# Four transformer layers on one core: the rotary exchange of the last layer by the vector engine's shuffle in place of four extra projections

## The chip, the core and the metric

One core of a Trainium2 chip. TensorE (PE in the profile; PEld is its weight load), VectorE (DVE), ScalarE (ACT), GpSimd (POOL) and SyncE (SP, which here only issues DMAs) run in parallel, each through its own instruction stream in program order; semaphores tie them together. Matmul results land in PSUM, which has eight banks. The metric is the device time of one execution in microseconds (us).

## The reference, cut to what matters

16 sequences of 256 tokens, 256 features, 16 heads of 16 features, go through four different transformer layers (0 to 3). All are: norm, modulation, attention, residual, norm, modulation, feed-forward, residual. Layer 3 is the only one that rotates queries and keys, and its feed-forward has two halves (gate and value), so twice the first product.

```python
def _rope(x):                       # layer 3, for q and for k, per head of 16
    ang = arange(T)[:, None] * inv_freq[None, :]
    x0, x1 = (x[..., 0::2], x[..., 1::2])
    o0 = x0 * cos - x1 * sin
    o1 = x1 * cos + x0 * sin
    return jnp.stack([o0, o1], axis=-1).reshape(x.shape)

qkv = x @ w_qkv + b_qkv
q, k, v = jnp.split(qkv, 3, axis=-1)
q = _rope(...q...); k = _rope(...k...)
attn = softmax(einsum('bhqd,bhkd->bhqk', q, k) / sqrt(hd))
out = einsum('bhqk,bhkd->bhqd', attn, v) ... @ w_ao + b_ao
...
a, gate = split(x @ w_fc + b_fc, 2); ffn = (a * silu(gate)) @ w_fo + b_fo
```

The rotation needs, for each feature, the value of its partner in the pair (2i, 2i+1).

## The kernel before

**Precision.** A product in float32 is made of three products of a high and a low part (hi*hi, hi*lo, lo*hi; the helper `product`, line L481). So each projection of 128 features (`project`) is 6 matmuls of 128x256, two 128-row pieces of the input times three. Names that end in h or l are such parts.

**Pipeline.** The unit of work is a tile: one sequence in one layer, 64 in all, layer by layer. One step t of the program works on five tiles at once, in different stages: n = t+2 (statistics and normalisation before attention), q = t+1 (norm to features, query, key and value projections), a = t (scores, softmax, outputs), r = t-1 (output projection, first residual, second norm), m = t-2 (feed-forward: `up`, activation, `down`, second residual). Every engine has a `body(s)` with the order of its work in a step written out by hand; there is no scheduler. The flag `rope` (on PE) and the tests `s.lq == ROPE` are true in the 16 steps t = 47 to 62, in which tile q is of layer 3; m is of layer 3 from t = 50 on.

**A step on PE.** First the front: eight rounds of `up(j)` and `down(j)` (feed-forward of m), with the output transposes, the output projection, and the score pairs 0 to 5 of tile a between them (a pair is two heads; L530). The front ends with `maxima_to_rows(0)` (L695). The rest of the step is called the tail here: `query`, `key`, the score pairs 6 and 7, then for eight pairs the transposed scores (`transposed_pair`, L724) which ACT turns into exponentials (L905), `values`, four groups of `outputs` (L747, each needs four heads' exponentials and the next set needs the banks that they free), and `norm_2` (transposes of the second norm, L590). Then the next step's `up(0)`.

**The rotation.** In layer 3, `query(f)` and `key(f)` project twice: once with the normal columns of the weights, once with columns in which each pair is swapped (columns 3*D and 4*D on), into banks 0 and 2 beside banks 1 and 3. `rotate` on DVE adds the biases and multiplies by cosine and signed sine (four SCALAR_TENSOR_TENSOR, L1157) into the buffer `G`; `split_rotated` adds the two products (L1168) and splits the sum into high (L1170) and low part (L1172) in `QHL` or `KHL`. SP then copies these into the stacked operands `QS` and `KS` of the scores by DMAs (L1345), 6 for each operand and group of heads. `G` is also the ring of the feed-forward's activations.

**Banks.** The bank of each head's score is in `S_BANKS`, of its transposed score in `ST_BANKS`, each with one table for layers 0 to 2 and one for layer 3, since there the swapped projections take banks 0 and 2. `NORM2_BANK` is that of `norm_2`. In the rope steps PE's transposed pair 0 writes banks 0 and 1, so it stands behind both projections and the rotation of the query, and `norm_2` waits for the rotation of the key.

**DVE in the tail**, rope steps: row maxima of the scores (`maxima`, L976, two instructions a pair), the multiplication or copy of the feed-forward's result (L1144), `rotate` of q, `statistics_2`, `split_rotated` of q, `rotate` of k, `normalise_2` (L956), `split_rotated` of k, `modulate_2` (L1094, L1100), `statistics_1` of tile n, evacuation of the outputs (L1108), `normalise_1` of n, the values (L1116).

## Time and profile before

| | |
|---|---|
| median of 3 runs | 2475.57 us (2473.37 to 2478.87) |
| profiled execution | 2480.4 us, of which span 2478.5 us |
| mean granted TensorE clock | 0.982 |
| PE / DVE / ACT / POOL busy | 93% / 66% / 51% / 44% |
| instructions | 63608 |

The profiled execution is one more run, 4.8 us above the median. The span is from its first to its last instruction. PE's busy share counts matmuls from issue to modelled end, and they overlap, so the distance between starts tells more than the share.

### The profile page before, as it was taken

How to read it: one execution, taken by the hardware profiler on the slowest of the kernel's cores; microseconds unless marked ns; L12 is line 12 of the kernel's file. 1: busy time of each engine (PE TensorE's matmuls, PEld its weight loads, DVE VectorE, ACT ScalarE, POOL GpSimd, SP SyncE). 2: the span in 40 equal slices, each digit the busy share in tenths (PEclk: the TensorE clock that was granted, in tenths of full speed). 3: DMA queues.
4: the chain of work that ended last, by engine and by line, in shares of the span. 5: the costliest groups of instructions: out<-in, count | busy, mean ns of one | idle time of the engine just before them, and what ended most of it. 6: DMA issues, size and time to landing. Idle time of an engine off the chain costs nothing.

```text
span 2478.5 us, 63608 instructions
## 1 busy us (share of the span) xinstructions
PE 2306.8 (93%) x20776; PEld 1908.5 (77%) x20776; DVE 1646.9 (66%) x3820; ACT 1255.5 (51%) x2624; POOL 1084.0 (44%) x1319
## 2 busy tenths in 40 slices
PE   6699999999999999999999999999999999999997
PEld 5477778877778778877777777777778787887876
DVE  3566676666665565556766676667777777677763
ACT  0366655566655554555666655566543433434332
POOL 1244444544544444444554444445534344343433
PEclk9799999999999999999999999999999999999988
DMA  6222121122211211122222211122221111111110
GB/s 211 84 67 69 63 61 61 59 71 80 90 63 57 66 59 51 61 69 78 86 79 67 68 57 58 60 70 84 64 82 45 63 51 50 65 42 60 52 53 14
DMA packets 165535, 166.66 MB, mean 67 GB/s; under 512 B 29392, under 2 KB 144976, under 8 KB 165424
## 3 DMA queue, kind: packets, MB, share of 16 engines
q1 hardware_dynamic: 165424, 165.21, 20.8%
q8 instruction: 65, 1.06, 0.2%
q14 instruction: 46, 0.38, 0.1%
HBM read 58.99 MB, written 4.39 MB: 26 GB/s over the span
## 4 chain that ended last, share of the span: by engine, by line
PE 47%; issue 20%; POOL 15%; DVE 10%; ACT 3%; SPq 1%; POOLq 1%; DMA 0%; DVEq 0%; ACTq 0%
PE B L481 20%; POOL GHl L1244 7%; PE B L581 7%; PE B L724 4%; PE B L530 4%; PE B L747 4%; PE B L506 3%; ACT PR L905 3%; DVE NEGM L976 2%; PE B L590 2%; POOL H1l L1283 2%; POOL X L1230 2%; POOL H2l L1270 1%; POOL X L1238 1%; PE B L600 1%
## 5 line engine op out<-in xcount | busy, mean ns | idle before, releaser
L905 ACT ACTIVATE PR<-B 128x512 f32<-128x512 f32 (+1 forms) x1024 | 508.4, 564 | 433.7 <-PE B L724 329.0
L1244 POOL TENSOR_TENSOR GHl<-G,GHh 128x256 fp32r<-128x256 f32 x512 | 376.5, 736 | 503.0 <-ACT GHh L878 332.1
L976 DVE TENSOR_REDUCE NEGM<-B 128x2 f32<-128x512 f32 x768 | 479.0, 683 | 78.7 <-PE B L530 78.0
L481 PE MATMUL B<-H2h,W1h 128*128 128x256 f32 x1280 | 394.5, 308 | 5.1 <-issue 3.1
L878 ACT ACTIVATE G<-B,VEC 128x256 f32<-128x256 f32 x384 | 182.1, 474 | 359.0 <-PE B L481 355.6
L481 PE MATMUL B<-H2h,W1l 128*128 128x256 f32 x1280 | 362.8, 283 | 0.0
L481 PE MATMUL B<-H2l,W1h 128*128 128x256 f32 x1280 | 362.3, 283 | 0.0
L747 PE MATMUL B<-PR,V 128*32 128x256 f32 (+1 forms) x4096 | 270.2, 383 | 62.8 <-ACT PR L905 62.1
L581 PE MATMUL B<-W2h,GHh 128*128 128x256 f32 x1024 | 299.2, 292 | 5.9 <-POOL GHl L1244 5.7
L581 PE MATMUL B<-W2l,GHh 128*128 128x256 f32 x1024 | 289.5, 283 | 0.0
L581 PE MATMUL B<-W2h,GHl 128*128 128x256 f32 x1024 | 288.7, 282 | 0.0
L481 PEld LDWEIGHTS B<-H2h,W1h 128*128 128x128 f32 x1280 | 244.3, 191 | 43.5 <-issue 30.4
L724 PE MATMUL B<-QS,KS 64*128 64x256 f32 (+1 forms) x2048 | 233.9, 320 | 13.6 <-ACT PR L905 8.7
L481 PEld LDWEIGHTS B<-H2l,W1h 128*128 128x128 f32 x1280 | 245.1, 192 | 0.0
L481 PEld LDWEIGHTS B<-H2h,W1l 128*128 128x128 f32 x1280 | 244.2, 191 | 0.0
L1270 POOL TENSOR_TENSOR H2l<-HF,H2h 128x512 fp32r<-128x512 f32 x64 | 81.9, 1279 | 371.1 <-DVE H2h L1100 371.1
L724 PEld LDWEIGHTS B<-QS,KS 64*128 64x128 f32 x2048 | 151.9, 189 | 116.7 <-issue 55.3
L747 PEld LDWEIGHTS B<-PR,V 128*32 128x32 f32 x4096 | 108.9, 111 | 168.9 <-ACT PR L905 103.0
L530 PE MATMUL B<-KS,QS 48*128 48x256 f32 (+1 forms) x2048 | 214.3, 315 | 15.5 <-DMA KS<-KHL 10.6
L581 PEld LDWEIGHTS B<-W2h,GHh 128*128 128x128 f32 x1024 | 195.4, 191 | 13.5 <-POOL GHl L1244 4.0
L530 PEld LDWEIGHTS B<-KS,QS 48*128 48x128 f32 x2048 | 144.5, 188 | 68.5 <-issue 14.5
L581 PEld LDWEIGHTS B<-W2l,GHh 128*128 128x128 f32 x1024 | 195.9, 191 | 0.0
(140 smaller groups left out, 4977.1 us busy)
## 6 DMA issues: line engine op xcount, KB each, us to landing
QS<-QHL SPq DMA_DIRECT2D x768, 64.0 KB, 2.1
KS<-KHL SPq DMA_DIRECT2D x768, 64.0 KB, 2.1
GA<-gate_scratch SPq DMA_DIRECT2D x48, 256.0 KB, 3.1
GM<-gate_scratch SPq DMA_DIRECT2D x48, 256.0 KB, 3.4
RAW<-in_w SPq DMA_DIRECT2D x36, 256.0 KB, 3.9
CW<-in_cw SPq DMA_DIRECT2D x3, 1536.0 KB, 13.8
X<-in_x SPq DMA_DIRECT2D x2, 2048.0 KB, 10.2
QS<-MT SPq DMA_DIRECT2D x256, 4.0 KB
```

The lines of the kernel that those rows point to most:

```text
L481: last = nc.tensor.matmul(dst, w[i], x[j], start=(first_k and n == 0), stop=(last_k and n == 2))
L506: return nc.tensor.matmul(dst, IDENTB[:], MASK[:, transposed], start=False, stop=True, skip_group_check=True)
L530: last = nc.tensor.matmul(bank(banks[h])[:, i, 0:keys], QS[b:b + STK, p, i * P:(i + 1) * P], KS[b:b + STK, p, 0:keys], start=(i == 0 or s. ...
L581: last = nc.tensor.matmul(bank(7)[:, i, :], GH[x][:, j % RING, i * P:(i + 1) * P], W2[y][:, j, :], start=(j == 0 and n == 0 and i == 0), s ...
L590: last = nc.tensor.transpose(dst[:, f, i * P:(i + 1) * P], src[:, i, f * P:(f + 1) * P], IDENT[:])
L724: last = nc.tensor.matmul(B[:, banks[h], k * T:k * T + T - first], KS[b:b + ROWS, p, k * P:(k + 1) * P], QS[b:b + ROWS, p, first:T], start ...
L747: last = nc.tensor.matmul(bank(6 + g // 2)[32 * j:32 * j + 32, g % 2, c], V[:, k, HV * h:HV * h + 32], PR[:, h % PRING, k, 0:n], start=(k ...
L878: last = nc.scalar.activation(dst[:, j % RING, :], bank(3 - j % 2)[:, 0, :], ACT.Gelu, bias=VEC[:, s.lm, V_B1 + j:V_B1 + j + 1])
L905: nc.scalar.activation(PR[:, h % PRING].rearrange("p k q -> p (k q)")[:, 0:n], src[:, 0:n], ACT.Exp, scale=SCALE).then_inc(ac_exp, 1)
L976: last = nc.vector.tensor_reduce(NEGM[:, :, c], src, op=ALU.max, axis=AX.X, negate=True)
L1244: nc.gpsimd.tensor_tensor(GH[1][:, j % RING, :], G[:, j % RING, :], GH[0][:, j % RING, :].bitcast(F32), ALU.subtract).then_inc(po_gl, 1)
L1270: nc.gpsimd.tensor_tensor(H2[1][:], HF[:], H2[0][:].bitcast(F32), ALU.subtract).then_inc(po_h2, 1)
```

## The change

The swapped projections go. In layer 3 `wq3` is as wide as in the other layers (768 columns, not 1280). `rotate` gets the partner of each feature from one STREAM_SHUFFLE of VectorE over the projection's PSUM bank (128x512); the partner of partition i is i XOR 4 (`HG` is 4), within groups of 32. Sine products then read the shuffled copy, in SBUF. The key's rotation has a buffer of its own (`GK`), and its sum (cosine part plus sine part) is made by GpSimd. The order of PE in a rope step and the banks become nearly those of layers 0 to 2; `norm_2` takes bank 7 and stands behind `outputs(1)`, and `values(1)` stands between `outputs(2)` and `outputs(3)`. On DVE `statistics_1` and `normalise_1` of layer 3's tiles move from the tail to the next step's rounds j = 1 and j = 4 of the feed-forward (with `rstd` on POOL at j = 2), `modulate_2` moves ahead of the key's rotation, and the key's split goes behind everything else. SP issues both groups of QS, then both of KS. The plan of weight loads has four chunks for `wq3` where there were eight, and step 47 loads no feed-forward weights any more.

```diff
-WQ_COLS = (3 * D, 3 * D, 3 * D, 5 * D)
+WQ_COLS = (3 * D,) * NL
...
-S_BANKS = ((4, 5, 0, 6) * 2 + (4, 5, 0, 2) * 2, (4, 5, 0, 6) * 2 + (4, 5, 2, 3) + (4, 5) * 2)
+S_BANKS = (4, 5, 0, 6) * 2 + (4, 5, 0, 2) * 2
 WO_BANK = 1
...
-ST_BANKS = ((4, 5, 0, 7) * 2 + (4, 5, 1, 3) * 2, (0, 1, 4, 5, 6, 7) + (0, 1, 4, 5) * 2 + (0, 1))
-NORM2_BANK = (0, 3)
+ST_BANKS = ((4, 5, 0, 7) * 2 + (4, 5, 1, 3) * 2, (4, 5, 0, 7) * 2 + (4, 5, 0, 1) * 2)
+NORM2_BANK = (0, 7)
+PARTNER = [i ^ HG for i in range(32)]
...
+                def key_read(s):
+
+                    if s.la >= ROPE:
+                        at_least(pe, dv_rot, 2 * (s.nq - NSEQ * ROPE))
+                    else:
+                        at_least(pe, dv_k, s.nq)
...
-                    if rope:
-                        pe.wait_ge(dv_rot, 2 * (s.q - NSEQ * ROPE) + 2)
-                    elif s.a is not None:
-                        pe.wait_ge(ac_exp, H * s.a + last_user(ST_BANKS[0][0:HB] + (0,), HB) + 1)
+                    if s.a is not None:
+                        pe.wait_ge(ac_exp, H * s.a + last_user(ST_BANKS[rope][0:HB] + (NORM2_BANK[rope],), HB) + 1)
...
                     last = project(bank(1)[:, f, :], cols(wq, f * P), H1)
-                    if rope:
-                        last = project(bank(0)[:, f, :], cols(wq, 3 * D + f * P), H1)
...
                     last = project(bank(3)[:, f, :], cols(wq, D + f * P), H1)
-                    if rope:
-                        last = project(bank(2)[:, f, :], cols(wq, 4 * D + f * P), H1)
...
+                        elif banks[h] == 1 and rope:
+                            pe.wait_ge(dv_rot, 2 * (s.q - NSEQ * ROPE) + 1)
...
+                        if rope and s.r is not None:
+                            pe.wait_ge(dv_f2, s.r + 1)
...
-                if rope:
-                    key(0)
-                    scores_if(7)
-                else:
-                    scores_if(7)
-                    key(0)
+                scores_if(7)
+                key(0)
                 key(1)
                 if s.a is not None:
                     transposed_pair(0)
-                    if not rope:
-                        transposed_pair(1)
+                    transposed_pair(1)
                     maxima_to_rows(1)
-                    if rope:
-                        transposed_pair(1)
-                    if not rope:
-                        values(0)
+                    values(0)
                     transposed_pair(2)
                     if not rope:
                         values(1)
                     transposed_pair(3)
                     outputs(0)
                     transposed_pair(4)
-                    if rope:
-                        values(0)
-                        transposed_pair(5)
-                        values(1)
-                    if s.r is not None:
+                    if s.r is not None and not rope:
                         norm_2()
-                    if not rope:
-                        transposed_pair(5)
+                    transposed_pair(5)
                     outputs(1)
+                    if s.r is not None and rope:
+                        norm_2()
                     transposed_pair(6)
                     transposed_pair(7)
                     outputs(2)
+                    if rope:
+                        values(1)
                     outputs(3)
...
+                    if j == 1 and s.lq == ROPE:
+                        statistics_1(s.q, s.sq, s.lq)
+                    if j == 4 and s.lq == ROPE:
+                        normalise_1(s.q, s.sq, s.lq, s.nq)
...
-                    rotate(s, pe_q, 1, 0, V_BQ, V_BQR, 0)
-                    maxima(7)
-                    statistics_2()
-                    split_rotated(s, QHL, dv_qh, dv_q, 0)
-                    rotate(s, pe_k, 3, 2, V_BK, V_BKR, 1)
+                    r = s.q - NSEQ * ROPE
+                    rotate(s, pe_q, 1, G, V_BQ, V_BQR, 0)
+                    dv.wait_ge(dv_rot, 2 * r + 1)
+                    nc.vector.tensor_tensor(G[:, 0:KD, :], G[:, 0:KD, :], G[:, KD:2 * KD, :], ALU.add).then_inc(dv_rot2, 1)
                     normalise_2()
-                    split_rotated(s, KHL, dv_kh, dv_k, 1)
+                    dv.wait_ge(dv_rot2, r + 1)
+                    split_rotated(s, G, QHL, dv_qh, dv_q)
+                    modulate_2()
+                    rotate(s, pe_k, 3, GK, V_BK, V_BKR, 1)
+                    evacuate(0)
+                    values_out()
+                    evacuate(1)
+                    dv.wait_ge(po_rot, r + 1)
+                    split_rotated(s, GK, KHL, dv_kh, dv_k)
...
-            def rotate(s, s_pe, nbank, nswap, vb, vbr, which):
-
+            def rotate(s, s_pe, nbank, dst, vb, vbr, which):
+
+                r = s.q - NSEQ * ROPE
                 dv.wait_ge(s_pe, s.q + 1)
-                if s.m is not None:
+                if which == 0 and s.m is not None:
                     dv.wait_ge(po_gl, NJ * s.m_done)
-                if which == 1:
-                    dv.wait_ge(dv_q, s.q + 1)
-                for c, nb, b in ((0, nbank, vb), (1, nswap, vbr)):
+                elif which == 1:
+                    at_least(dv, dv_k, s.nq)
+                apart(dv)
+                nc.vector.stream_shuffle(dst[:, KD:2 * KD, :], bank(nbank), PARTNER).then_inc(dv_swap, 1)
+                for c, b in ((0, vb), (1, vbr)):
+                    if c == 1:
+                        dv.wait_ge(dv_swap, 2 * r + which + 1)
                     for f in range(KD):
-                        last = nc.vector.scalar_tensor_tensor(G[:, 2 * c + f, :], bank(nb)[:, f, :],
-                                                              VEC[:, ROPE, b + f:b + f + 1], ROT[:, c, :],
-                                                              ALU.add, ALU.mult)
+                        src = dst[:, KD + f, :] if c else bank(nbank)[:, f, :]
+                        last = nc.vector.scalar_tensor_tensor(dst[:, KD * c + f, :], src, VEC[:, ROPE, b + f:b + f + 1],
+                                                              ROT[:, c, :], ALU.add, ALU.mult)
                 last.then_inc(dv_rot, 1)
 
-            def split_rotated(s, dst, s_hi, s_lo, which):
-
-                r = s.q - NSEQ * ROPE
+            def split_rotated(s, src, dst, s_hi, s_lo):
+
                 for group in range(2):
                     at_least(dv, sp_stk[group], STACKED * s.nq)
-                dv.wait_ge(dv_rot, 2 * r + which + 1)
-                nc.vector.tensor_tensor(G[:, 0:2, :], G[:, 0:2, :], G[:, 2:4, :], ALU.add).then_inc(dv_rot2, 1)
-                dv.wait_ge(dv_rot2, 2 * r + which + 1)
-                nc.vector.tensor_copy(dst[:, 0], G[:, 0:2, :]).then_inc(s_hi, 1)
+                nc.vector.tensor_copy(dst[:, 0], src[:, 0:KD, :]).then_inc(s_hi, 1)
                 dv.wait_ge(s_hi, s.q + 1)
-                nc.vector.tensor_tensor(dst[:, 1], G[:, 0:2, :], dst[:, 0].bitcast(F32), ALU.subtract).then_inc(s_lo, 1)
+                nc.vector.tensor_tensor(dst[:, 1], src[:, 0:KD, :], dst[:, 0].bitcast(F32), ALU.subtract).then_inc(s_lo, 1)
...
+                    if j == 2 and s.lq == ROPE:
+                        rstd(MV1, RS1, TV1, dv_mv1, po_t1, po_rs1, s.q, s.lq)
...
+                if s.lq == ROPE:
+                    r = s.q - NSEQ * ROPE
+                    po.wait_ge(dv_rot, 2 * r + 2)
+                    nc.gpsimd.tensor_tensor(GK[:, 0:KD, :], GK[:, 0:KD, :], GK[:, KD:2 * KD, :], ALU.add).then_inc(po_rot, 1)
...
+                    by_group = [(QS, 0), (KS, 0), (QS, 1), (KS, 1)]
+                    by_operand = [(QS, 0), (QS, 1), (KS, 0), (KS, 1)]
+                    for dst, group in by_operand if s.lq == ROPE else by_group:
...
-    w3 = g["L3_cond_w_qkv"]
-    def stacked(q, k, v, *rotated):
-        return np.concatenate([q[:, paired], k[:, paired], v, *(w[:, swap][:, paired] for w in rotated)], axis=1)
...
-    d["wq3"] = stacked(*np.split(w3, 3, axis=1), w3[:, 0:D], w3[:, D:2 * D])
+    d["wq3"] = stacked(*np.split(g["L3_cond_w_qkv"], 3, axis=1))```

PE, the end of a rope step (t = 62), from transposed pair 5 to the last `outputs`; before:

```order
L724 MATMUL B<-QS,KS 128x256 x4
L481 MATMUL B<-WQ1h,H1h 128x256
L481 MATMUL B<-WQ1l,H1h 128x256
L481 MATMUL B<-WQ1h,H1l 128x256
L481 MATMUL B<-WQ1h,H1h 128x256
L481 MATMUL B<-WQ1l,H1h 128x256
L481 MATMUL B<-WQ1h,H1l 128x256
L590 MATMUL B<-IDENT,TOK 128x128 x4
L747 MATMUL B<-PR,V 32x256 x8
L724 MATMUL B<-QS,KS 128x256 x8
L747 MATMUL B<-PR,V 32x256 x16
```

and of the change, from transposed pairs 4 and 5 on (L716 is L724 of before, L741 is L747, L596 is L590, L482 is L481):

```order
L716 MATMUL B<-QS,KS 128x256 x8
L741 MATMUL B<-PR,V 32x256 x8
L596 MATMUL B<-IDENT,TOK 128x128 x4
L716 MATMUL B<-QS,KS 128x256 x8
L741 MATMUL B<-PR,V 32x256 x8
L482 MATMUL B<-WQ1h,H1h 128x256
L482 MATMUL B<-WQ1l,H1h 128x256
L482 MATMUL B<-WQ1h,H1l 128x256
L482 MATMUL B<-WQ1h,H1h 128x256
L482 MATMUL B<-WQ1l,H1h 128x256
L482 MATMUL B<-WQ1h,H1l 128x256
L741 MATMUL B<-PR,V 32x256 x8
```

The six matmuls of `values(1)` have moved from ahead of `outputs(1)` to between `outputs(2)` and `outputs(3)`, and `norm_2` is behind `outputs(1)`.

DVE, the same step, from the query's rotation to the key's split; before:

```order
L1157 SCALAR_TENSOR_TENSOR G<-B,VEC,ROT 128x256 x4
L976 TENSOR_REDUCE NEGM<-B 128x2 x2
L945 BN_STATS ST<-X 128x6 x2
L950 BN_AGGR MV<-ST 128x2 x2
L1168 TENSOR_TENSOR G<-G 128x512
L1170 CAST QHL<-G 128x512
L1172 TENSOR_TENSOR QHL<-G,QHL 128x512
L1157 SCALAR_TENSOR_TENSOR G<-B,VEC,ROT 128x256 x4
L956 TENSOR_SCALAR TOK<-X,RS 128x256 x2
L1168 TENSOR_TENSOR G<-G 128x512
L1170 CAST KHL<-G 128x512
L1172 TENSOR_TENSOR KHL<-G,KHL 128x512
```

and of the change, from the query's shuffle to the copy of the values (the key's split, L1170 and L1172, comes behind the next copy of outputs):

```order
L1156 STREAM_SHUFFLE G<-B 128x512
L1162 SCALAR_TENSOR_TENSOR G<-B,VEC,ROT 128x256 x2
L1162 SCALAR_TENSOR_TENSOR G<-G,VEC,ROT 128x256 x2
L1117 TENSOR_TENSOR G<-G 128x512
L941 TENSOR_SCALAR TOK<-X,RS 128x256 x2
L1170 CAST QHL<-G 128x512
L1172 TENSOR_TENSOR QHL<-G,QHL 128x512
L1087 TENSOR_SCALAR HF<-B,COND 128x256 x2
L1093 CAST H2h<-HF 128x512
L1156 STREAM_SHUFFLE GK<-B 128x512
L1162 SCALAR_TENSOR_TENSOR GK<-B,VEC,ROT 128x256 x2
L1162 SCALAR_TENSOR_TENSOR GK<-GK,VEC,ROT 128x256 x2
L1101 COPY OR<-B 128x512
```

All four maxima of pairs 6 and 7 and the statistics now stand ahead of the query's rotation, and the second norm's modulation (L1087, L1093) has moved from behind both splits to between the query's split and the key's rotation.

## Rows read from the trace of the kernel before

**Rows 1.** The page, section 1: busy us, share of the span, instructions.

```profile
PE 2306.8 (93%) x20776; PEld 1908.5 (77%) x20776; DVE 1646.9 (66%) x3820; ACT 1255.5 (51%) x2624; POOL 1084.0 (44%) x1319
```

**Rows 2.** Windows, step lengths: busy of PE, PEld, DVE, ACT, POOL; clock; DMA.

```profile
1939.93:1983.29 43.36, 40.73 (x370) 34.93 (x369) 32.60 (x73) 17.42 (x34) 17.81 (x23) 1.00 0.17 55
2161.09:2205.47 44.38, 42.09 (x370) 35.60 (x369) 32.61 (x73) 17.42 (x34) 17.82 (x23) 0.96 0.16 54
2338.62:2384.37 45.75, 43.53 (x370) 36.88 (x369) 31.02 (x68) 17.41 (x34) 16.36 (x19) 0.93 0.18 55
```

**Rows 3.** Windows, four tails: steps 53, 47, 58 and, last, 42 (layer 2).

```profile
1960.43:1980.31 19.88, 17.41 (x173) 12.54 (x170) 16.03 (x36) 9.84 (x19) 6.42 (x11) 1.00 0.20 67
1709.22:1728.83 19.61, 17.39 (x173) 12.51 (x170) 14.97 (x35) 10.87 (x21) 7.87 (x11) 1.00 0.23 69
2181.57:2202.48 20.91, 18.78 (x173) 13.21 (x170) 16.03 (x36) 9.84 (x19) 6.41 (x11) 0.92 0.21 67
1537.66:1553.26 15.60, 13.73 (x146) 9.46 (x146) 12.75 (x32) 9.97 (x19) 5.49 (x7) 1.00 0.23 77
```

**Rows 4.** Timeline of PE, step 53: start, us, engine, line, work, count [idle <-releaser].

```profile
1949.24 0.74 PE L530 MATMUL B<-KS,QS 48*128 48x256 f32 x8
...
1961.60 0.28 PE L481 MATMUL B<-H1h,WQ1h 128*128 128x256 f32 x1
...
1963.04 0.28 PE L481 MATMUL B<-H1h,WQ1h 128*128 128x256 f32 x1
...
1967.60 0.50 PE L724 MATMUL B<-QS,KS 64*128 64x256 f32 x4
...
1979.31 1.07 PE L747 MATMUL B<-PR,V 128*32 128x256 f32 x16 [0.99 <-ACT PR L905]
```

**Rows 5.** Timeline of PE, the tail of a layer 2 step (t = 42).

```profile
1541.55 0.74 PE L724 MATMUL B<-QS,KS 64*128 64x256 f32 x8
```

**Rows 6.** Timeline of ACT in the rope tail of rows 4: exponentials.

```profile
1968.22 0.60 ACT L905 ACTIVATE PR<-B 128x512 f32<-128x512 f32 x1 [7.06 <-PE B L724]
...
1968.98 3.43 ACT L905 ACTIVATE PR<-B 128x512 f32<-128x512 f32 x7
...
1977.19 2.06 ACT L905 ACTIVATE PR<-B 128x512 f32<-128x512 f32 x4 [1.77 <-PE B L724]
```

**Rows 7.** Timeline of DVE in the same tail.

```profile
1962.13 0.67 DVE L1144 COPY TOK<-B 128x512 f32<-128x512 f32 x1
...
1966.79 1.28 DVE L976 TENSOR_REDUCE NEGM<-B 128x2 f32<-128x512 f32 x2
1967.99 0.74 DVE L945 BATCH_NORM_STATS2 ST<-X 128x6 f32 x2
...
1969.15 0.69 DVE L1168 TENSOR_TENSOR G<-G 128x512 f32<-128x512 f32 x1
1969.88 0.43 DVE L1170 CAST QHL<-G 128x512 fp32r<-128x512 f32 x1
...
1971.17 1.66 DVE L1157 SCALAR_TENSOR_TENSOR G<-B,VEC,ROT 128x256 f32<-128x256 f32 x4
1972.74 0.61 DVE L956 TENSOR_SCALAR TOK<-X,RS 128x256 f32 x2
...
1975.93 1.00 DVE L1094 TENSOR_SCALAR HF<-B,COND 128x256 f32<-128x256 f32 x2 [0.79 <-PE B L590]
...
1978.36 0.69 DVE L1108 COPY OR<-B 128x512 f32<-128x512 f32 x1
...
1982.71 0.48 DVE L983 SCALAR_TENSOR_TENSOR G<-B,VEC,G 128x256 f32<-128x256 f32 x1 [0.47 <-ACT G L872]
```

**Rows 8.** Timeline of POOL there.

```profile
1977.53 1.27 POOL L1270 TENSOR_TENSOR H2l<-HF,H2h 128x512 fp32r<-128x512 f32 x1 [5.61 <-DVE H2h L1100]
```

**Rows 9.** Timeline of SP's queue, and the page's section 6 (last: us to landing).

```profile
1983.28 3.73 SPq L1345 DMA_DIRECT2D KS<-KHL  x6
...
KS<-KHL SPq DMA_DIRECT2D x768, 64.0 KB, 2.1
```

More of the change, by code:

```diff
@@ L509, in score_pair @@
                 def score_pair(p):
[L511 removed]
+                    a_, banks = s.a, S_BANKS
                     if p == 0:
@@ L1024, in outputs_lo, with statistics_1, normalise_1 @@
                     last.then_inc(dv_ot, 1)
+                def statistics_1(tile, sequence, layer):
+                    if isinstance(tile, int) and tile == 4:
+                        dv.wait_ge(sp_x[1], 16)
+                    if layer > 0:
+                        dv.wait_ge(po_x2, tile - (NSEQ - 1))
+                    statistics(tokens(sequence), ST1, MV1, dv_st1, dv_mv1, tile)
+                def normalise_1(tile, sequence, layer, before):
+                    dv.wait_ge(po_rs1, tile + 1)
+                    at_least(dv, pe_h1, before)
+                    normalise(XQ, tokens(sequence), MV1, RS1, dv_xn1, layer == ROPE)
                 for j in range(NJ):
@@ L1131, in body @@
                     normalise_2()
-                modulate_2()
-                statistics_1()
-                evacuate(0)
-                if s.n is not None:
-                    dv.wait_ge(po_rs1, s.n + 1)
-                    at_least(dv, pe_h1, s.q_done)
-                    normalise(XQ, tokens(s.sn), MV1, RS1, dv_xn1, s.ln == ROPE)
-                values_out()
-                evacuate(1)
+                    modulate_2()
+                    if s.n is not None and s.ln != ROPE:
+                        statistics_1(s.n, s.sn, s.ln)
+                    evacuate(0)
+                    if s.n is not None and s.ln != ROPE:
+                        normalise_1(s.n, s.sn, s.ln, s.q_done)
+                    values_out()
+                    evacuate(1)
             def multiply(s, src, rows, s_rows, n, layer):
```

98 lines of the change are left out of this document (40 added, 58 removed).

## The prediction

> **What bounds the kernel now.** I read the page first: PE is busy 93% of the span, no other engine over 66% [rows 1]. So whatever takes matmuls away can pay, but the busy share hides waits, since matmuls overlap. The second view is a table of windows, one for each step, cut at the output transposes. The change touches the tails of steps 47 to 62 (and little of their fronts). These last 43.36 us at full clock (four of them, t = 50 to 53) and about 44.4 us in the eight steps after (t = 54 to 61), where the granted clock is 0.96: a tail of 20.91 us at 0.92 [rows 3] means some 3.4 us at the lower level, 1.2 GHz; the last one, t = 62, lasts 45.75 us at 0.93 [rows 2]. The third view cuts out the tail alone, from the end of the first maxima transposes to the next step's first feed-forward matmul: 19.88 us at full clock, 20.91 us with a fall of the clock, 19.61 us in step 47, and 15.60 us in layer 2, whose tail has the same work but for the 24 swapped projection matmuls [rows 3]. PE's work in both is less than their length: in the rope tail it stands 0.99 us for exponentials before the last outputs alone [rows 4], and ACT stands 7.06 us until the first transposed scores are there and 1.77 us more before its last four exponentials [rows 6]. The tail is a chain, projections, transposed scores, exponentials, outputs, and its start is late in a rope step.
>
> **The matmuls.** Twelve matmuls of this form take 1.44 us, 0.12 us each (start to start, 1961.60 to 1963.04) [rows 4]. 24 of them a step are 2.88 us, over 16 steps 46 us. None of it lies beside other work: all stand between the end of the front and the first transposed pair, which starts 7.17 us after the tail's begin (1967.60 less 1960.43) and 3.89 us in layer 2 (1541.55 less 1537.66) [rows 3 to 5]. I take 3.9 for the change, since its order there is that of layer 2.
>
> **The chain on ACT.** The first exponential starts 0.62 us after the first transposed scores (1968.22 less 1967.60), so at 4.5; seven take 3.43 us, 0.49 each [rows 4, 6]. With the copy of the maxima (0.26, from 1968.22 + 0.50 to 1968.98) eight are done at 4.5 + 8 x 0.49 + 0.26 = 8.7. Pairs 4 and 5 now follow each other behind the first outputs, so the next four run to about 10.9. Pair 6 stands behind `norm_2`, at about 10.6, so the last four start at 11.2 and end at 13.3. The last outputs take 1.00 us (1979.31 to the tail's end at 1980.31) [rows 3, 4]. On this chain alone the tail would end at 14.3. The wait of 1.77 us is gone, since the values no longer stand between pairs 4 and 6.
>
> **The chain on DVE.** This is the new danger, so I add it up. The copy of the feed-forward result ends 2.3 us into the tail (1962.13 + 0.67, less overlap, less 1960.43); the maxima of a pair take 1.20 us (1966.79 to 1967.99), so both are done at 4.7; the statistics take 1.16 us (to 1969.15), to 5.9 [rows 7]. Then comes the shuffle. **The trace of before has none.** From below, its nearest row is a copy of the same 128x512 from PSUM to SBUF on the same engine, 0.69 us [rows 7]; from above, GpSimd's operation over 128x512, 1.27 us [rows 8]. I take 0.72, by the copy, which has the same source, destination and size, and keep 1.27 for the range; a gain below the copy I exclude, as no row of DVE over 512 float32 from PSUM is shorter. The Trainium skill (VectorE: DVE Perf Modes, the perf-mode tier table) gives STREAM_SHUFFLE one mode only, about 2400 ns for 2048 elements; a quarter of that, an estimate by that page, is 0.6 us, and the sum would be the same within 0.1 us a shuffle.
>
> So: shuffle to 6.6, four multiplications 1.57 (1971.17 to 1972.74) to 8.2, sum 0.73 to 9.0, `normalise_2` 0.55 to 9.5, the query's split 0.46 + 0.83 (1969.88 to 1971.17) to 10.8 [rows 7]. `modulate_2` needs `norm_2` of PE, done about 10.8, and takes 1.0: 11.9. PE's third outputs now wait for it (bank 7), then 1.0, `values(1)` 0.92, the last outputs 1.0: **14.9**. DVE meanwhile does the cast (0.4), the key's shuffle and four multiplications (2.3): 14.7, which `up(0)` waits for (bank 3). Both chains end together, and that on ACT 0.6 us before. Layer 2's measured tail is 15.6. I take 15.2, between the reckoned 14.9 and the measured 15.6.
>
> **What costs nothing, and its cover.** The key's sum leaves DVE (0.69) for POOL (1.27 [rows 8]); POOL idles 5.61 us just before in that tail, and the sum is hidden by the three evacuations, three times 0.6, that DVE does meanwhile; without that cover it would cost 0.6. The key's split ends at 14.7 + 1.8 + 1.2 = 17.7, that is 2.8 us into the next front. Behind it on DVE is the activation of round 0, which in the old step starts 2.4 us after `up(0)` (1982.71 less 1980.31) [rows 7]: 0.5 us late, against idle time of about that size before rounds 0 and 1. `statistics_1` (1.2) and `normalise_1` (0.6) lie in rounds 1 and 4, where DVE waits for ACT or PE: its busy time in a step is 32.60 of 43.36 us [rows 2], and with two shuffles more and one sum less 33.3 of some 38.7, still 5 us idle. `up(1)` waits for the values' copy, at 14.7 + 1.2 = 15.9, while `up(0)` lasts 1.5 us where m is of layer 3, but 0.8 us in the first three steps. I allow 0.3 us a step for all this.
>
> **DMAs.** KS is now copied last: its first six transfers are issued from 17.7, take 3.73 us and land 2.1 us after issue [rows 9], at about 23. The first scores stand 12.3 us behind their step's `up(0)` (1949.24 less 1936.95, which is 1980.31 less a step of 43.36 [rows 2 to 4]), so at 27.5; in the first three steps five rounds of `up` ahead of them are 6 matmuls shorter each, 3.6 us, so at 23.9. Slack is 4.5 and 0.9 us. The fewer weight chunks and the removed split of layer 3's weights on DVE in step 47 are other engines' work in idle time; I count nothing.
>
> **The sum.** Full clock, four steps: 19.88 - 15.2 = 4.7, 18.8 us. Eight steps with a fall: 20.91 - 15.2 = 5.7, if the fall goes with the thin stretch, 45.6. The last, 45.75 - 43.36 = 2.4 more than a full-clock step: 7.1. The first three: 19.61 - 15.2 = 4.4, 13.2. Together 84.7, less 16 x 0.3 = 4.8: **80 us**. The profiled execution's 2480.4 gives 2400; it lies 4.8 above the median of the runs shown, 2475.57, from which I predict 2396.
>
> **The clock, row against rule.** In this trace the clock fell in steps whose waits on PE are about 1 us (0.99 [rows 4]), at full clock in four steps with the same work, at 0.96 in eight [rows 2]. By these rows a fall can come in the new tail as well, at 20.91 - 19.88 = 1.03 us each [rows 3]; layer 2's tail, at 1.00, had none. The Trainium skill (TensorE: Matmul & The Clock Gate, Part 1) says that a warm array falls to half only after an idle window; by that rule nothing in either kernel should fall, and the gain would not contain a change of clock. The rows differ from it, so the rule bears no number here.
>
> **Rivals.**
> *The clock falls in the new steps too*, once in each of the 13 with layer 3's feed-forward: 13 us given back, 2409. For it: eight falls in a row before. Against it: a shorter, denser tail like layer 2's. 12%.
> *The shuffle is dear*, 1.27 us: 0.55 twice on DVE's chain, 1.1 us a step, 18 us: 2414. For it: no row has it. 8%.
> *Only the matmuls go*: the distance from the first transposed pair to the next step stays 12.7 us (1967.60 to 1980.31) [rows 3, 4] instead of 11.3, because DVE's longer chain takes the place of ACT's waits: 46 us, 2430. 8%.
> *Shorter still*: the allowance is not needed and the tail is 14.7, (0.5 + 0.3) x 16 = 13 us more, 2383. That belongs to the forecast's own spread.
> *Slower than before*: DVE's chain becomes the bound. Each us on the shuffle puts 2 us on the key's rotation, which `up(0)` awaits. The gain of 80 us, 5 a step, is used up at 2.5 us more a shuffle, a price of 3.2 us, more than four copies. At 3.7 us it would be 2475 + 16 = 2491. Nothing in the rows speaks for it but the absence of a row. 2%.
>
> **How the numbers follow.** The forecast (2383 to 2405) has 68%, the clock 12, the dear shuffle 8, the matmuls alone 8, slower 2, no change 2. To hold 8 in 10, the range goes from 2383 to 2416, the forecast, the clock and the dear shuffle without their sum. What a measurement can tell from no change is 0.2%, 5 us. Faster has 0.96, same 0.02, slower 0.02.
>
> **What would show it.** In the changed profile: STREAM_SHUFFLE x32 at about 0.7 us; tails near 15.2 us and rope steps near 38.8 with layer 3's feed-forward; the first transposed pair 3.9 us into the tail; no wait of 1.77 us before the last exponentials; the third outputs waiting for DVE (HF) under 0.5 us; no scores waiting for KS in steps from 50 on. The prediction is wrong if fronts grow (DVE late in rounds 0 to 4), if `up(0)` or `up(1)` waits over 1 us for DVE, or if the clock column stays below 1.00.

## The result, and the profile after

The changed kernel takes **2400.07 us**, median of 4 runs (2393.51 to 2402.58), against 2474.47 us for the kernel before (4 runs, 2470.27 to 2478.87). The ratio is 0.9688, interval 0.967 to 0.9705. The profiled execution took 2402.53 us with a span of 2400.7 us, where the one of before had 2480.4 and 2478.5. So 78 us went between the profiled executions and 74 between the medians, where 80 had been forecast for both.

The page of the kernel after: its first section, the clock in 40 slices, and the group of the exponentials, the one part of ACT on which the argument turned.

```profile
span 2400.7 us, 63280 instructions
PE 2240.4 (93%) x20392; PEld 1859.2 (77%) x20392; DVE 1660.3 (69%) x3866; ACT 1254.3 (52%) x2620; POOL 1089.8 (45%) x1333
...
PEclk9899999999999999999999999999999999999998
...
L890 ACT ACTIVATE PR<-B 128x512 f32<-128x512 f32 (+1 forms) x1024 | 506.7, 564 | 339.1 <-PE B L716 230.6
```

PE has 384 matmuls fewer than in [rows 1], which is 24 in each of 16 steps, and 66 us less of busy time; its share is still 93%. DVE has 13 us more.

The windows view, cut as in [rows 2, 3]: first the step t = 47 and its tail, then t = 50, t = 58, t = 62, and last the tail of t = 58. Columns: length, busy time of PE, PEld, DVE, ACT and POOL, granted clock, DMA share, GB/s.

```profile
1695.61:1729.53 33.92, 31.68 (x298) 26.35 (x297) 27.71 (x59) 20.17 (x43) 17.53 (x22) 1.00 0.19 60
1712.88:1727.84 14.96, 13.82 (x150) 9.64 (x147) 13.35 (x32) 10.30 (x20) 3.96 (x6) 1.00 0.20 60
1799.21:1838.74 39.53, 37.61 (x347) 32.16 (x345) 36.76 (x81) 19.65 (x38) 18.06 (x24) 1.00 0.22 68
2112.58:2151.65 39.07, 37.32 (x346) 32.13 (x345) 33.38 (x77) 17.43 (x34) 18.03 (x24) 1.00 0.18 61
2268.91:2307.57 38.66, 37.33 (x347) 32.10 (x346) 33.24 (x77) 17.43 (x34) 18.03 (x24) 1.00 0.19 61
2133.46:2148.67 15.21, 13.84 (x149) 9.66 (x146) 13.89 (x33) 10.29 (x20) 4.18 (x7) 1.00 0.18 60
```

The tail has gone from 19.88 us (20.91 with a fall of the clock) to 15.21 us, and the clock stands at 1.00 in every rope step. Where the step of 45.75 us at 0.93 stood [rows 2], one of 38.66 stands.

Three timelines of that last tail show its chains. PE (start, us, engine, line, work, count, and in brackets the idle time before with its releaser):

```profile
2131.21 0.50 PE L530 MATMUL B<-KS,QS 48*128 48x256 f32 x4
2132.08 0.50 PE L530 MATMUL B<-KS,QS 48*128 48x256 f32 x4 [0.37 <-DVE NEGM L961]
...
2137.38 0.74 PE L716 MATMUL B<-QS,KS 64*128 64x256 f32 x8
...
2139.64 0.50 PE L716 MATMUL B<-QS,KS 64*128 64x256 f32 x4 [0.32 <-ACT PR L890]
2140.59 0.50 PE L716 MATMUL B<-QS,KS 64*128 64x256 f32 x4 [0.45 <-ACT PR L890]
...
2143.70 0.66 PE L596 MATMUL B<-IDENT,TOK 128*128 128x128 f32 x4
2144.28 1.07 PE L716 MATMUL B<-QS,KS 64*128 64x256 f32 x8
2145.77 1.07 PE L741 MATMUL B<-PR,V 128*32 128x256 f32 x16 [0.41 <-DVE HF L1087]
```

The first transposed pair starts 3.92 us into the tail (2137.38 less 2133.46), where it was 7.17. The third outputs wait 0.41 us for `modulate_2` (HF), and pairs 2 and 3 of the transposed scores wait 0.32 and 0.45 us for exponentials, which free their banks. The first two rows belong to the front: the second half of score pair 5 waits 0.37 us for a maximum.

ACT, its exponentials, which answer to [rows 6]:

```profile
2137.99 0.60 ACT L890 ACTIVATE PR<-B 128x512 f32<-128x512 f32 x1 [3.80 <-PE B L716]
...
2142.64 2.07 ACT L890 ACTIVATE PR<-B 128x512 f32<-128x512 f32 x4 [0.29 <-PE B L716]
2144.89 2.06 ACT L890 ACTIVATE PR<-B 128x512 f32<-128x512 f32 x4 [0.19 <-PE B L716]
```

The wait of 7.06 us is 3.80 and the one of 1.77 us is 0.19. DVE, which answers to [rows 7]:

```profile
2139.11 0.73 DVE L1156 STREAM_SHUFFLE G<-B 128x512 f32<-128x512 f32 x1
2139.74 0.85 DVE L1162 SCALAR_TENSOR_TENSOR G<-B,VEC,ROT 128x256 f32<-128x256 f32 x2
...
2144.63 1.00 DVE L1087 TENSOR_SCALAR HF<-B,COND 128x256 f32<-128x256 f32 x2 [0.93 <-PE B L596]
...
2146.01 0.74 DVE L1156 STREAM_SHUFFLE GK<-B 128x512 f32<-128x512 f32 x1
...
2147.43 0.87 DVE L1162 SCALAR_TENSOR_TENSOR GK<-GK,VEC,ROT 128x256 f32<-128x256 f32 x2
```

The shuffle takes 0.73 to 0.75 us, and the next instruction starts 0.63 after it does. What the prediction did not have is the 0.93 us that DVE stands before `modulate_2`, for PE's `norm_2` (L596): DVE's part up to the query's split was done 0.56 us sooner than reckoned. The key's rotation ends at 2148.3, and `up(0)` starts at 2148.67.

### The profile page after: what moved, and what is told of

Same layout as the page of the kernel before. It is cut to its first block, busy times and chain, and to the rows that moved or that the text cites. A ratio compares the mean times of both kernels' runs of the same rounds, so it can differ in the third digit from the quotient of the medians.

```text
span 2400.7 us, 63280 instructions
## 1 busy us (share of the span) xinstructions
PE 2240.4 (93%) x20392; PEld 1859.2 (77%) x20392; DVE 1660.3 (69%) x3866; ACT 1254.3 (52%) x2620; POOL 1089.8 (45%) x1333
## 4 chain that ended last, share of the span: by engine, by line
PE 58%; issue 14%; POOL 10%; DVE 9%; ACT 4%; SPq 1%; POOLq 1%; DMA 0%; DVEq 0%; ACTq 0%
PE B L482 25%; PE B L587 8%; PE B L741 6%; PE B L530 5%; PE B L716 5%; POOL GHl L1244 5%; PE B L507 3%; PE B L596 3%; ACT PR L890 3%; DVE NEGM L961 3%; PE B L606 1%; POOL H1l L1289 1%; POOL X L1230 1%; PE B L689 1%; DVE HF L1087 1%
## 5 line engine op out<-in xcount | busy, mean ns | idle before, releaser
L890 ACT ACTIVATE PR<-B 128x512 f32<-128x512 f32 (+1 forms) x1024 | 506.7, 564 | 339.1 <-PE B L716 230.6
L961 DVE TENSOR_REDUCE NEGM<-B 128x2 f32<-128x512 f32 x768 | 477.7, 683 | 61.2 <-PE B L530 60.4
L482 PE MATMUL B<-H2h,W1h 128*128 128x256 f32 x1280 | 394.8, 308 | 3.2 <-issue 3.1
L482 PE MATMUL B<-H2h,W1l 128*128 128x256 f32 x1280 | 362.9, 283 | 0.0
L482 PE MATMUL B<-H2l,W1h 128*128 128x256 f32 x1280 | 362.4, 283 | 0.0
L741 PE MATMUL B<-PR,V 128*32 128x256 f32 (+1 forms) x4096 | 261.3, 373 | 36.3 <-ACT PR L890 29.4
L482 PEld LDWEIGHTS B<-H2h,W1h 128*128 128x128 f32 x1280 | 244.5, 191 | 41.5 <-issue 21.4
L716 PE MATMUL B<-QS,KS 64*128 64x256 f32 (+1 forms) x2048 | 229.3, 315 | 29.3 <-ACT PR L890 27.2
L716 PEld LDWEIGHTS B<-QS,KS 64*128 64x128 f32 x2048 | 153.5, 186 | 120.2 <-ACT PR L890 75.3
L482 PEld LDWEIGHTS B<-H2l,W1h 128*128 128x128 f32 x1280 | 245.3, 192 | 0.0
L482 PEld LDWEIGHTS B<-H2h,W1l 128*128 128x128 f32 x1280 | 244.5, 191 | 0.0
L530 PE MATMUL B<-KS,QS 48*128 48x256 f32 (+1 forms) x2048 | 214.1, 315 | 21.8 <-DMA KS<-KHL 11.0
L741 PEld LDWEIGHTS B<-PR,V 128*32 128x32 f32 x4096 | 108.3, 109 | 131.9 <-ACT PR L890 65.8
L530 PEld LDWEIGHTS B<-KS,QS 48*128 48x128 f32 x2048 | 144.8, 188 | 75.1 <-issue 20.6
## 6 DMA issues: line engine op xcount, KB each, us to landing
X<-in_x SPq DMA_DIRECT2D x2, 2048.0 KB, 10.2
```

Of the source, the lines that this page charges most:

```text
L482: last = nc.tensor.matmul(dst, w[i], x[j], start=(first_k and n == 0), stop=(last_k and n == 2))
L530: last = nc.tensor.matmul(bank(banks[h])[:, i, 0:keys], QS[b:b + STK, p, i * P:(i + 1) * P], KS[b:b + STK, p, 0:keys], start=(i == 0 or s. ...
L716: last = nc.tensor.matmul(B[:, banks[h], k * T:k * T + T - first], KS[b:b + ROWS, p, k * P:(k + 1) * P], QS[b:b + ROWS, p, first:T], start ...
L741: last = nc.tensor.matmul(bank(6 + g // 2)[32 * j:32 * j + 32, g % 2, c], V[:, k, HV * h:HV * h + 32], PR[:, h % PRING, k, 0:n], start=(k ...
L890: nc.scalar.activation(PR[:, h % PRING].rearrange("p k q -> p (k q)")[:, 0:n], src[:, 0:n], ACT.Exp, scale=SCALE).then_inc(ac_exp, 1)
L961: last = nc.vector.tensor_reduce(NEGM[:, :, c], src, op=ALU.max, axis=AX.X, negate=True)
```

## The experiments

Nine kernels, in four questions. Single runs of one kernel differ by 1 to 16 us. In the profiled executions the stretch ahead of step t = 47, in which the kernels do nearly the same work, took anything from 1686 to 1696 us; why it differs is open. So besides the ratios I compare two lengths that leave it out: one rope step with layer 3's feed-forward, and the sum of the 16 rope steps, each from one profiled execution (from the output transposes of t = 47 to those of t = 63).

| kernel | median us | 16 rope steps | one step | rope steps with a fall of the clock |
|---|---|---|---|---|
| before | 2473.86 to 2478.51 | 692.5 | 43.36 | 9 |
| after | 2400.07 | 612.0 | 39.07 | 0 |
| shuffle, old order | 2492.28 | 707.7 | 44.07 | 16 |
| the same, matmuls back | 2491.48 | 707.9 | 44.60 | 5 |
| new order, matmuls back | 2441.93 | 655.6 | 41.80 | 0 |
| each shuffle twice | 2412.46 | 623.3 | 39.70 | 0 |
| no shuffle | 2398.57 | 611.7 | 39.09 | 0 |
| values early | 2397.0 | 613.7 | 39.14 | 0 |
| pair 5's banks | 2393.09 | 609.0 | 38.82 | 0 |
| key's sum on DVE | 2398.99 | 615.0 | 39.23 | 0 |
| pair 5's banks and `norm_2` early | 2392.23 | 602.5 | 38.30 | 0 |

**1. Which part of the change bears the gain?**

*The shuffle without the new order:* the kernel before, with the swapped projections replaced by the shuffle, while the order on PE and DVE and all banks stay as they were.

```diff
                     last = project(bank(1)[:, f, :], cols(wq, f * P), H1)
-                    if rope:
-                        last = project(bank(0)[:, f, :], cols(wq, 3 * D + f * P), H1)
...
-                for c, nb, b in ((0, nbank, vb), (1, nswap, vbr)):
+                nc.vector.stream_shuffle(G[:, KD:2 * KD, :], bank(nbank), PARTNER).then_inc(dv_swap, 1)
+                for c, b in ((0, vb), (1, vbr)):
...
+                        src = G[:, KD + f, :] if c else bank(nbank)[:, f, :]
```

Expected: 

> The kernel before with one part of the change alone: the swapped projections replaced by the shuffle, and order, banks, buffers and DMA order of before kept. Theory (chain): the gain is half matmuls, half order. The first transposed pair still waits for the query's rotation, which now holds a shuffle and stands behind the maxima of pair 6, so it starts about 5.8 us into the tail (7.2 before, 3.9 after) and the rest of the tail stays 12.7 us: tail 18.5, about 1.4 us less a step, some 2450 us. Rival (matmul count): each step is shorter by all 24 matmuls, 2.9 us, tail 17.0, some 2430 us, and the order adds the rest.

Measured: 2492.28 us (9 runs) against 2478.51 (16 runs), ratio 1.0064 (1.0043 to 1.0084). With 384 matmuls fewer it is *slower* than before, where both theories had it faster. Its windows: one rope step, the tail of that step, and the stretch of the tail until the clock falls and at the lower level.

```profile
2125.47:2169.54 44.07, 40.09 (x347) 33.62 (x346) 33.76 (x77) 17.59 (x34) 17.72 (x23) 0.92 0.17 54
2145.95:2166.55 20.60, 16.79 (x149) 11.23 (x146) 17.20 (x40) 10.01 (x19) 6.32 (x11) 0.83 0.22 68
2145.95:2153.27 7.32, 5.16 (x41) 4.01 (x38) 7.32 (x16) 0.97 (x2) 1.51 (x2) 1.00 0.16 37
2153.27:2160.10 6.83, 6.18 (x42) 4.02 (x40) 6.37 (x17) 4.85 (x10) 2.36 (x4) 0.50 0.24 78
```

The same tail on PE's timeline, the rows with a wait and one between them:

```profile
2149.57 0.50 PE L531 MATMUL B<-KS,QS 48*128 48x256 f32 x4 [0.60 <-DVE NEGM L973]
...
2151.77 0.50 PE L721 MATMUL B<-QS,KS 64*128 64x256 f32 x4 [0.79 <-DVE G L1159]
2153.05 0.40 PE L692 MATMUL B<-IDENT,NEGM 128*8 128x128 f32 x2 [0.77 <-DVE NEGM L973]
2153.38 1.81 PE L721 MATMUL B<-QS,KS 64*128 64x256 f32 x12
2155.84 1.93 PE L744 MATMUL B<-PR,V 128*32 128x256 f32 x16 [0.65 <-ACT PR L902]
...
2165.55 1.07 PE L744 MATMUL B<-PR,V 128*32 128x256 f32 x16 [1.00 <-ACT PR L902]
```

The first transposed pair starts 5.82 us in, as the first theory had it. It needs a bank that DVE's rotation frees, and DVE has no slack in this order: in its first 7.32 us DVE is busy for 7.32, and PE for only 5.16. Then the clock falls for 6.83 us (sixteen matmuls of the outputs take 1.93 us there and 1.07 at full clock), and the wait for the last exponentials is still there. Every rope step from t = 47 on has such a fall, of 6.8 or 10.2 us, where before had 3.4 us in eight steps and 6.8 in one. Over the 16 steps the times add up to 707.7 us against 692.5 of before, 15 us more; the medians differ by 14.

*The same with the matmuls put back,* each projection of a query and key computed twice:

```diff
                     last = project(bank(1)[:, f, :], cols(wq, f * P), H1)
+                    if rope:
+                        last = project(bank(1)[:, f, :], cols(wq, f * P), H1)
```

(and likewise for the key, bank 3). Expected: 

> The kernel of e1 (shuffle alone, old order) with query() and key() each done twice into the same bank in layer 3, so with the 24 matmuls a step back. Theory (e1 is slow because PE stands for DVE where the matmuls were and its clock falls for it): the matmuls fill those waits, the first transposed pair starts 7.8 us into the tail at full clock, tail 20.5, falls as rare as before: 2480 to 2490 us, not slower than e1 (2492) with 384 matmuls more. Rival (e1 is slow through DVE's longer chain alone, the clock is no cause): 24 matmuls at 0.12 come on top of e1 at least in part, 2510 to 2538 us.

Measured: 2491.48 us (4 runs) against 2475.16, ratio 1.0084 (1.0058 to 1.0109). It is the same time as without them. Its step and tail:

```profile
2124.38:2168.98 44.60, 40.70 (x371) 34.92 (x369) 33.84 (x77) 17.53 (x34) 17.72 (x23) 1.00 0.15 50
2144.84:2165.98 21.14, 17.39 (x173) 12.52 (x170) 17.30 (x40) 9.95 (x19) 6.34 (x11) 1.00 0.19 63
```

and the two places of that tail at which PE now waits for DVE, on its timeline:

```profile
2153.25 0.38 PE L696 MATMUL B<-IDENT,NEGM 128*8 128x128 f32 x2 [0.73 <-DVE NEGM L977]
...
2158.57 0.39 PE L482 MATMUL B<-WQ1h,H1h 128*128 128x256 f32 x1 [1.07 <-DVE G L1163]
```

At clock 1.00 the step is 44.60, 1.2 us above the 43.36 of [rows 2]: that is what the shuffle costs in the old order, through DVE: the wait of 1.07 us for the key's rotation was 0.35 in the kernel before, and the one of 0.73 us wasn't there. Five of the 16 rope steps show a fall. Theory had 2480 to 2490 us and is missed by a little; its rival, 2510 to 2538, is far off. Taking the 24 matmuls away makes the step 44.07 at 0.92. The first transposed pair then starts 1.36 us sooner (5.82 against 7.18 us in), PE standing for DVE where the other matmuls were, and the rest of the tail is 0.82 us longer (14.78 against 13.96), most of the fall lying in it. So 0.5 us of 2.9 is left in this step, and over the run nothing.

*The new order with the matmuls put back:* the kernel after, with the same duplicated projections.

Expected: 

> The changed kernel with query() and key() each done twice into the same bank in layer 3: the 24 matmuls a step of before are back, order, banks and shuffle as changed. Theory: all of them lie ahead of the first transposed pair, tail 18.1, steps 42.0, 46 us more: 2446 us; what is left against 2475, 30 us, is what order and clock gave. Rival (the order gave nothing, matmuls and clock all): 2475 us.

Measured: 2441.93 us (4 runs) against 2473.86, ratio 0.9859 (0.9839 to 0.988).

```profile
2140.62:2182.42 41.80, 40.16 (x370) 35.03 (x369) 33.37 (x77) 17.34 (x34) 18.07 (x24) 1.00 0.18 57
```

A step is 41.80, 2.73 us above that of after (24 x 0.114), with no fall in the rope steps; theory had 42.0 and 2446 us. So the change divides: the order, banks and shuffle with the matmuls kept give 32 us between medians (2473.86 less 2441.93; 35 by the ratio), of which the step shows 1.6 us at full clock (43.36 to 41.80) and 1.0 us more where the clock fell; the matmuls give the remaining 42 us (2441.93 less 2400.07; 42 by the two ratios as well). By the sums of the 16 steps it is 37 and 44 us.

Four of the kernels have one shuffle for the query and one for the key and differ in two things alone (in the old order the swapped columns of the weights are still loaded). Medians in us:

| | matmuls kept | matmuls away |
|---|---|---|
| old order | 2491.48 | 2492.28 |
| new order | 2441.93 | 2400.07 |

The new order is worth some 50 us with the matmuls (52 by the 16 steps) and some 92 without (96); taking the matmuls away is worth nothing in the old order and 42 us in the new. Neither has a worth of its own. Which part of the new order (PE's, DVE's, the banks or the buffer `GK`) bears most of the 50 us was not tested.

**2. Do the shuffles cost anything?**

*Each shuffle twice:*

```diff
                 nc.vector.stream_shuffle(dst[:, KD:2 * KD, :], bank(nbank), PARTNER).then_inc(dv_swap, 1)
+                dv.wait_ge(dv_swap, 4 * r + 2 * which + 1)
+                apart(dv)
+                nc.vector.stream_shuffle(dst[:, KD:2 * KD, :], bank(nbank), PARTNER).then_inc(dv_swap, 1)
...
```

Expected: 

> The changed kernel with each STREAM_SHUFFLE done twice, one after the other. Theory (DVE's chain sets the tail's end since the third outputs wait 0.4 us for HF): the query's second shuffle, 0.64 us, goes straight to the tail, the key's adds 0.3 more at up(0): tails 15.8 to 16.2, 10 to 15 us more than the change, about 2413 us. Rival (PE or ACT bound, DVE has room): nothing, 2400 us.

Measured: 2412.46 us (4 runs), ratio 0.9732 (0.9702 to 0.9762). The number came out as the theory had it; PE's timeline of a tail shows that the way was another:

```profile
2153.48 1.07 PE L741 MATMUL B<-PR,V 128*32 128x256 f32 x16 [0.46 <-DVE HF L1087]
...
2156.95 0.39 PE L482 MATMUL B<-H2h,W1h 128*128 128x256 f32 x1 [0.49 <-DVE GK L1165]
```

The wait for HF is 0.46 instead of 0.41, so the query's second shuffle (0.86 us with its gap) vanished in DVE's wait of 0.93. The key's reached `up(0)` with 0.49 of its 0.86. The tail is 15.81.

*No shuffle:* the rotation multiplies each feature itself where its partner belongs.

```diff
-                nc.vector.stream_shuffle(dst[:, KD:2 * KD, :], bank(nbank), PARTNER).then_inc(dv_swap, 1)
...
-                        src = dst[:, KD + f, :] if c else bank(nbank)[:, f, :]
+                        src = bank(nbank)[:, f, :]
```

Expected: 

> The changed kernel without the shuffles: the sine products read the projection's bank itself, so the rotation uses each feature instead of its partner. Theory: 0.64 us earlier HF takes away only the wait of 0.4 us, then PE is the bound: tail 14.8, 6 us less than the change, about 2394 us. Rival (DVE is the bound all along): 1.3 us a step, 20 us less, 2380 us. Rival (PE bound already): no change.

Measured: 2398.57 us (4 runs), ratio 0.9678 (0.9647 to 0.9709). The step is unchanged, 39.09, as the last rival had it and not as theory had. DVE's timeline says why:

```profile
2137.97 0.99 DVE L1087 TENSOR_SCALAR HF<-B,COND 128x256 f32<-128x256 f32 x2 [1.58 <-PE B L596]
```

The query's shuffle is gone and DVE waits 0.65 us longer for `norm_2`, so that PE's wait for HF is still 0.41. **In the new order the two shuffles cost nothing.** They stand in slack, 0.93 us for the query's and 0.37 us ahead of `up(0)` for the key's (2148.67 less 2148.30).

**3. What are the waits that are left in the new step?**

*The values ahead of pair 3, as in other layers:* `values(1)` for rope steps moved back from behind `outputs(2)`.

```diff
-                    if not rope:
-                        values(1)
+                    values(1)
                     transposed_pair(3)
...
-                    if rope:
-                        values(1)
                     outputs(3)
```

Expected: 

> The changed kernel with values(1) between transposed pairs 2 and 3, as in layers 0 to 2. Theory: PE waits 0.7 us for exponentials there, which the 0.9 us of matmuls fill; the last outputs then start when the last exponential is done (0.2 us after 2146.95 in the trace) or the key's rotation ends (2148.3): tail 14.8 to 14.9, 5 us less than the change, 2395 us. Rival: the place behind outputs(2) hides the wait for HF and for the last exponentials, so the move gains nothing or costs: 2400 to 2405 us.

Measured: 2397.0 us (6 runs), ratio 0.9673 (0.965 to 0.9697), which does not tell it from the kernel after; the step is 39.14 (+0.07) and the 16 steps 1.7 us more, so by the steps the rival holds. The wait of 0.45 us for exponentials is gone, the wait for HF stays, and `up(0)` then waits 0.27 us for the key's rotation: six matmuls earlier leave PE early at a place where it has to wait for DVE.

*Score pair 5 in other banks:*

```diff
-S_BANKS = (4, 5, 0, 6) * 2 + (4, 5, 0, 2) * 2
+S_BANKS = ((4, 5, 0, 6) * 2 + (4, 5, 0, 2) * 2, (4, 5, 0, 6) * 2 + (4, 5, 2, 3) + (4, 5, 0, 2))
...
```

(with the waits that go with it). Expected: 

> The changed kernel with the banks of score pair 5 as before (2 and 3, not 0 and 2) in the rope steps; key() then waits for that pair's maxima. Theory: in the changed kernel pair 5 waits 0.4 us for the maximum of head 6, since both use bank 0, and the rest of the step is late by it; the banks give back 0.4 us a step: steps 38.7 instead of 39.07, 6 us less than the change, 2394 us. Rival: down(7) waits for POOL's GHl right behind (0.2 us in the trace of before), so the wait only moves: 2400 us.

Measured: 2393.09 us (5 runs) against 2473.86, ratio 0.9678 (0.9657 to 0.9699); the step is 38.82, 0.25 less, where theory had 0.4. The pair's 8 matmuls are in one piece again, and the front is 0.37 us shorter (38.82 less a tail of 15.33 is 23.49, against 23.86); the tail is 0.12 longer, since the maxima's transposes in it now wait 0.17 us. Between medians it can't be told from after.

*The key's sum on DVE:*

```diff
+                    dv.wait_ge(dv_rot, 2 * r + 2)
+                    nc.vector.tensor_tensor(GK[:, 0:KD, :], GK[:, 0:KD, :], GK[:, KD:2 * KD, :], ALU.add).then_inc(po_rot, 1)
```

(and out of POOL). Expected: 

> The changed kernel with the key's sum on VectorE, ahead of its split, instead of on GpSimd. Theory: it delays DVE's round 0 of the next front by 0.6 us, to 3.2 us behind up(0), and up(2) needs it at 3.8: covered, 0 to 2 us more than the change. Rival: DVE is tight at the start of the front, each step is 0.6 us longer: 2410 us.

Measured: 2398.99 us (4 runs), ratio 0.9696 (0.9674 to 0.9718); the step is 39.23 to 39.30, 0.2 us longer; over the 16 steps that is 3 us, near theory's 0 to 2. The sum took 0.95 us in its place on DVE (middle of 16), where the query's took 0.69; POOL's copy of the values ran beside it for 0.4 us. PE feels 0.2 of the 0.95.

**4. Can the named waits be taken away?**

The banks of pair 5, and `norm_2` ahead of `outputs(1)`, so that `modulate_2` can begin earlier:

```diff
                     transposed_pair(5)
-                    outputs(1)
                     if s.r is not None and rope:
                         norm_2()
+                    outputs(1)
```

Expected: 

> The changed kernel with two edits: pair 5's banks as in e5, and norm_2 ahead of outputs(1) instead of behind it. Theory: modulate_2 waits for PE's norm_2 (DVE idle 0.93 us), not for DVE's own work, so norm_2 a microsecond earlier takes away the wait of the third outputs for HF (0.4 us) and lets the key's rotation end earlier: 0.4 + 0.4 us a step, steps 38.3, 12 us less than the change, about 2388 us. Rival: the third outputs wait for exponentials anyway, only the banks give something: 2394 us.

Measured: **2392.23 us** (5 runs, 2391.72 to 2392.68) against 2473.86, ratio 0.9662 (0.9647 to 0.9678), the best of all. Its step and tail:

```profile
2106.19:2144.49 38.30, 37.17 (x347) 32.02 (x346) 33.35 (x76) 17.43 (x34) 18.05 (x24) 1.00 0.19 62
2126.66:2141.51 14.85, 13.87 (x149) 9.64 (x146) 14.64 (x34) 9.96 (x19) 4.88 (x8) 1.00 0.18 59
```

On PE's timeline its third outputs follow their predecessors without a wait:

```profile
2136.66 1.07 PE L744 MATMUL B<-PR,V 128*32 128x256 f32 x16
2137.67 1.00 PE L719 MATMUL B<-QS,KS 64*128 64x256 f32 x8
2138.60 1.07 PE L744 MATMUL B<-PR,V 128*32 128x256 f32 x16
```

The step is 0.77 us shorter than in the kernel after, 38.3 as theory said, and the 16 steps together 9.5 us, where it had 12. The median doesn't tell theory's 2388 from the rival's 2394 well; the rival's reason, that the third outputs wait for exponentials anyway, is refuted by the rows. The 0.41 us for HF, which pair 5's banks alone left at 0.41, is gone by moving PE's transposes and not by shortening DVE. PE is now busy 37.17 of 38.30 us; its longest stands are the 0.32 and 0.45 us for exponentials, which no experiment here took away together with these.

## Why the prediction was right, and where its steps were not

**The matmuls.** Foreseen: 0.12 us each, 2.88 a step, all of it on the path, 46 us. With the order held fixed they are 2.73 a step and 42 us. The unspoken part is the condition: in the old order the same 384 matmuls are worth nothing. The price was right and the sentence beside it, "None of it lies beside other work", holds for the new order alone.

**The tail.** Foreseen 15.2, measured 15.21 (14.96 at t = 47); the first transposed pair 3.9 us in, measured 3.92; the wait of 1.77 us gone, measured 0.19. That 15.2 was hit to a hundredth is luck: it was taken between the chains' 14.9 and layer 2's measured 15.6 [rows 3], and the measured tail lies 0.3 from the one and 0.4 from the other.

**The chain on DVE.** The price of the shuffle, 0.72, was right (0.73 to 0.75); its place in the sum was not. The prediction had `modulate_2` ready to start "about 10.8" by both DVE and PE. DVE was there at 10.24 us (2143.70) and then stood for PE's `norm_2`, whose modelled end is at 10.90, so `modulate_2` started at 11.17 (2144.63). The third outputs so began at 12.31 and not at 11.9, and from there on the sum held (1.0, 0.9 and 1.0 us): these 0.4 us are what lies between 14.9 and 15.21. So the 0.41 us that PE stands for HF go back to PE's own order, in which `norm_2` comes late. Without shuffles nothing changed, with two of each 0.6 us did: the query's shuffle would have begun to cost only above 1.6 us. The rival *the shuffle is dear* was overpriced: by the same slacks, as an estimate, 0.55 us more on each shuffle would have gone into the query's 0.93 whole, and of the key's 0.18 (0.55 less 0.37) would have reached `up(0)`, which is 3 us over the run and not 18. The last rival's threshold, 2.5 us more a shuffle, stays untried.

**The allowance.** 0.3 us a step was right in size (the front went from 43.36 - 19.88 = 23.48 to 39.07 - 15.21 = 23.86, 0.38 more) and wrong in cause. DVE is not late in rounds 0 and 1, and no scores wait for KS. It is score pair 5: bank 0 for head 6 is shared again, as in the other layers, and its second half waits 0.37 us for a maximum. Giving it the banks that before had for it brought the front back to 23.49 us and the step down by 0.25. The diff shows this bank; the prediction put no price on it.

**The steps one by one.** The first three gave 14.5 us (12.3 foreseen, after the allowance), the next four 16.2 (17.6), the eight with a fall of the clock 42.7 (43.2), the last 7.1 (6.8); together 80.5 against 79.9. That the whole agrees better than its parts is luck. In the first two steps a wait of 0.42 us that `up(1)` had for the values' copy went as well, which the prediction had down as a risk and not as a gain. The step t = 50 is 39.53 and not 39.07, with four instructions more on DVE, which is busy for 36.76 us of it; score pair 5 waits 0.67 us there. Ahead of these steps the execution took 3.7 us longer than that of before, behind them 1 us less; that makes the 77.8 us between the spans. These stretches have the old work, and I didn't look for the cause of their difference by an experiment.

**The clock.** The rival that the new steps fall too didn't come: 1.00 in all of them. Across the kernels it goes with the order: none of the eight in the new order (after and seven experiments) has a fall in a rope step, with or without the 24 matmuls, and the longest stand of PE in each of their tails is 0.3 to 0.6 us. In the old order it is 0.9 to 1.2 us, and falls came in 9, 16 and 5 of 16 steps (before, the shuffle alone, the shuffle with the matmuls). Whether it is the stands or something else in the order that decides was not tested, and what sets a single fall off is not settled: before had none in four steps and one in each of the next eight, with the same work [rows 2]. The Trainium skill (TensorE: Matmul & The Clock Gate, Part 1) has the clock fall after an idle window; the trace differs, for the longest stand of PE in the 7.32 us ahead of the fall shown is 0.79 us. The prediction's "only" goes beyond the page: the same part of the Trainium skill also tells of a clock that goes up and down where TensorE idles briefly but often between groups of matmuls. These rows are nearer to that, with stands of 0.60 to 0.79 us ahead of a fall. The forecast took the lost 1.0 us a step as recovered, with a chance against it, and it was; it had no mechanism for that, only layer 2's tail at 1.00 as a model.

**Only the matmuls go.** The rival (2430) had DVE's longer chain take ACT's place. Its mechanism exists, but in the old order: there, together with the lower clock, it takes as much as the matmuls give and more.

## What to carry to other kernels

Work taken off the bounding engine pays only where the order lets the engine's next work come forward: test the order and the removal apart, since here, with the shuffle in each, both together gave 74 us, the order with the matmuls kept 32, and the removal in the old order lost 14. When a helper engine gets the work instead, look for the wait that it already has ahead of the next instruction that others need; a chain summed without it prices the work at its full duration, where its cost may be nothing. If another stage of the same program already runs in the order that is planned, put its measured length beside the sum of durations: here they bounded the result from above and below (15.6 and 14.9 for 15.21).
